# Perceiver block on one core: two mixtures of experts with three float32r products for each fp32 product

## The reference

```python
# stage 5: x is the normalised input, 8 experts, one for each row
logits = x @ gate_w.T
top_v = jnp.max(logits, axis=-1); sel = jnp.argmax(logits, axis=-1)
rw = jax.nn.sigmoid(top_v)
for e in range(n_exp):
    xs = x * (rw * (sel == e))[:, None]
    out = out + (xs @ w_up[e].T) * jax.nn.silu(xs @ w_gate[e].T) @ w_down[e].T

# stage 8: 8 routed experts (two for each row) and 2 shared ones
def _expert(xf, w1, w3, w2):
    return jax.nn.silu(xf @ w1) * (xf @ w3) @ w2
gates = softmax of the two largest logits of each row, 0 elsewhere
out = sum_e gates[:, e] * _expert(xf, routed e) + sum of the two shared experts
```

## Time and profile before

| | |
|---|---|
| median of 3 runs | 1501.59 us (1499.80 to 1501.68) |
| the profiled execution | 1503.77 us, its span 1502.0 us |
| TensorE busy | 95% of the span |
| mean granted TensorE clock | 0.987 of full speed |
| stage 5 (normalisation to the last down) | about 518 to 575 us of the span |
| stage 8 | about 777 to 847 us |

### The profile page before, as it was taken

The page is one execution under the profiler, slowest core; times in us unless marked ns, Lnnn a source line. Parts: engine busy times, 40 slices in busy tenths (PEclk is TensorE's granted clock), DMA queues, the critical chain, the costliest instruction groups (busy, mean ns, idle before and its releaser), DMA issues.

```text
span 1502.0 us, 26221 instructions
## 1 busy us (share of the span) xinstructions
PE 1430.5 (95%) x10513; PEld 979.6 (65%) x10513; DVE 967.1 (64%) x1667; ACT 750.2 (50%) x1379; POOL 331.2 (22%) x439
## 2 busy tenths in 40 slices
PE   7899999999999999999999989999989899999998
PEld 4797666887888655898565545555545454555697
DVE  4776645544787534787363378889989892567533
ACT  5574342113665424664442337777777676325232
POOL 3784340002643213642103041110000000100000
PEclk9999999999999999999999999999999999999999
DMA  9314132221212410211315365545757412310140
GB/s 373 129 57 181 63 121 92 95 85 36 73 69 107 151 59 35 91 57 55 106 70 186 51 173 92 85 76 87 177 79 146 93 20 106 161 57 2 57 169 14
DMA packets 43008, 147.74 MB, mean 98 GB/s; under 512 B 6380, under 2 KB 21996, under 8 KB 34028
## 3 DMA queue, kind: packets, MB, share of 16 engines
q1 hardware_dynamic: 42888, 146.07, 33.7%
HBM read 123.49 MB, written 22.56 MB: 97 GB/s over the span
## 4 chain that ended last, share of the span: by engine, by line
PE 83%; DVE 9%; ACT 4%; issue 2%; POOL 2%; DMA 0%; SPq 0%; ACTq 0%; POOLq 0%; DVEq 0%
PE PS L163 51%; PE PS L2399 8%; PE PS L2311 7%; PE PS L2296 5%; PE PS L634 2%; PE PS L1660 2%; DVE SM L2415 2%; PE PS L1889 1%; POOL CNr L932 1%; PE PS L1910 1%; PE PS L2390 1%; PE PS L2985 1%; PE PS L1917 1%; PE PS L2890 1%; DVE SM L306 1%
## 5 line engine op out<-in xcount | busy, mean ns | idle before, releaser
L2415 DVE TENSOR_REDUCE SM<-PS 128x1 f32<-128x1024 f32 x256 | 301.8, 1219 | 42.4 <-PE PS L2296 41.1
L163 PE MATMUL PS<-ARr 128*128 128x256 f32 (+1 forms) x672 | 177.2, 323 | 0.8 <-POOL CNr L932 0.8
L2311 PE MATMUL PS<-AR 49*128 49x256 bf16 (+1 forms) x1216 | 162.9, 271 | 1.1 <-DVE AR L2436 0.7
L163 PE MATMUL PS<-HT,AR 128*128 128x512 f32 x328 | 153.4, 616 | 2.6 <-ACT HT L355 1.1
L163 PE MATMUL PS<-CNr,ARr 128*128 128x256 f32 x672 | 130.7, 292 | 11.6 <-DVE ARr L801 10.7
L2311 PE MATMUL PS<-AR,CT 49*128 49x256 bf16 (+1 forms) x832 | 124.6, 272 | 0.0
L163 PE MATMUL PS<-ARr,HTr 128*128 128x512 f32 x384 | 122.3, 400 | 0.5 <-issue 0.5
L163 PEld LDWEIGHTS PS<-ARr 128*128 128x128 f32 x672 | 114.9, 190 | 10.1 <-issue 1.2
L862 ACT CAST ARr<-PS 128x512 fp32r<-128x512 f32 x96 | 56.3, 586 | 112.5 <-PE PS L634 112.5
L163 PEld LDWEIGHTS PS<-HT,AR 128*128 128x128 f32 x328 | 61.4, 195 | 78.0 <-issue 74.1
L163 PE MATMUL PS<-AR 128*128 128x256 f32 (+3 forms) x504 | 109.5, 371 | 1.4 <-DVE AR L720 0.8
(11 more groups left out here) (403 smaller groups left out, 2727.7 us busy)
## 6 DMA issues: line engine op xcount, KB each, us to landing
CN<-ctx_n SPq DMA_DIRECT2D x24, 1024.0 KB, 5.6
AR<-k_parts SPq DMA_DIRECT2D x114, 128.0 KB
k_parts<-CN SPq DMA_DIRECT2D x32, 384.0 KB, 3.3
CT<-pack SPq DMA_DIRECT2D x6, 2048.0 KB, 7.6
AR<-pack SPq DMA_DIRECT2D x20, 512.0 KB, 4.6
CT<-k_parts SPq DMA_DIRECT2D x78, 128.0 KB
CT<-ctx_t SPq DMA_DIRECT2D x8, 1024.0 KB, 19.1
v_ones<-CN SPq DMA_DIRECT2D x28, 288.0 KB, 3.0
```

The lines of the kernel that those rows point to most:

```text
L163: last = te.matmul(o, l, r, start=first and k == 0, stop=final and k == n - 1, skip_group_check=True)
L2311: return te.matmul(PS[:, b, z * 256:z * 256 + 256], keys[rows, c * 128:c * 128 + 128], QQ9[rows, pr, rest, cols], start=not rest, stop=boo ...
L2415: ve.tensor_reduce(MX9[:, p % 2, e, g % 8 // 4, g % 4:g % 4 + 1], PS[:, b:b + 2, :].rearrange("p a b -> p (a b)"), AX, ALU.max).then_inc(* ...
```

## The change

In both mixtures gate, up and down of each expert become three float32r products: head of the weight by head of the rows, head by rest, rest by head. Gate 0, up 0 and the last down stay fp32.

- ScalarE casts HT to float32r (HTH) after its half of the turned rows; VectorE subtracts (HTR, two operations) before it copies the logits.
- For gate and up of expert e ScalarE casts both weights (`head_gate_up`, to GUH), and VectorE subtracts (`rest_gate_up`; the rest is written over the weight, W and WR being the same place). For down the same with `head_down` (DH) and `rest_down`.
- For the hidden rows ScalarE casts HB to HBH (in the space of H), and VectorE subtracts to HBR, over HB, at the end of its part for e.
- TensorE's gate e now waits for `gur` e and `htr`, down e for `hr` e and `dr` e.
- Ahead of its loop VectorE does `rest_gate_up` 1, then copies the gate rows, then `rest_down` 0 and `rest_gate_up` 2. ScalarE does `head_gate_up` 1, `head_down` 0, `head_gate_up` 2 at the start of its part.

```diff
-        CT = sb("CT", [128, 2, 8192])
-
         def both(name, shape):
 
             with nc.sbuf_tensor(name, shape, F32) as a:
                 pass
             return a, sb(name + "r", shape, F32R)
 
+        CT, CTr = both("CT", [128, 2, 8192])
         CN, CNr = both("CN", [128, 64, 256])
         X = sb("X", [128, 4, 256])
-        H = sb("H", [128, 4, 256])
+        H, Hr = both("H", [128, 4, 256])
...
-        def experts(s, W, n, n_gated, R, RT, work, gate_first):
+        def experts(s, W, WR, n, n_gated, R, RT, work, gate_first, HTH, HTR, GUH, DH):
             RB = [view(AR, work + 512 * k, 512) for k in range(2)]
             GB = [view(AR, work + 1024 + 512 * k, 512) for k in range(2)]
             HB = [view(AR, work + 2048 + 512 * k, 512) for k in range(3)]
+            HBR = [view(ARr, work + 2048 + 512 * k, 512) for k in range(3)]
+            HBH = [view(Hrf, 512 * k, 512) for k in range(2)]
 
             row_gone = lambda e: ("h", s, "up" if gate_first else "row", e)
             gate_gone = lambda e: ("h", s, "gated" if gate_first else "up", e)
             ready = lambda e: ("h", s, "gated" if gate_first else "row" if e < n_gated else "up", e)
+            late = lambda e: ("late", s) if e >= 5 and not gate_first else ("w", s)
             esel, idb = W["esel"].bitcast(BF16), W["idb"].bitcast(BF16)
+            gu = lambda e, k: mat(GUH[e % 2][:, 256 * k:256 * k + 256], 2)
 
             def pe_part(pe):
                 te = pe.e
 
+                def hidden(e, kind, k, gone):
+                    b, before = PB.take((kind, s, e), gone)
+                    pe.wait_ge(*before, *ht_all(s))
+                    w, o = mat(W[f"{kind}{e}"], 2), PS[:, b, :]
+                    if e == 0:
+                        last = mm(te, o, [(w[:, kt, :], HT[:, kt, :]) for kt in range(2)])
+                    else:
+                        pe.wait_ge(("gur", s, e), ("htr", s))
+                        wh, wr = gu(e, k), mat(WR[f"{kind}{e}"], 2)
+                        last = mm(te, o, [p for kt in range(2) for p in (
+                            (wh[:, kt, :], HTH[:, kt, :]), (wh[:, kt, :], HTR[kt]), (wr[:, kt, :], HTH[:, kt, :]))])
+                    last.then_inc(*pe.inc("expert", kind + "_ps", s, e))
+
                 def gate(e):
-                    wg = mat(W[f"g{e}"], 2)
-                    b, before = PB.take(("g", s, e), ("g", s, e))
-                    pe.wait_ge(*before, *ht_all(s), ("late", s) if e >= 5 and not gate_first else None)
-                    mm(te, PS[:, b, :], [(wg[:, kt, :], HT[:, kt, :]) for kt in range(2)]).then_inc(
-                        *pe.inc("expert", "g_ps", s, e))
+                    hidden(e, "g", 0, ("g", s, e))
 
                 def up(e):
-                    wu = mat(W[f"u{e}"], 2)
-                    b, before = PB.take(("u", s, e), ("h", s, "up", e))
-                    pe.wait_ge(*before)
-                    mm(te, PS[:, b, :], [(wu[:, kt, :], HT[:, kt, :]) for kt in range(2)]).then_inc(
-                        *pe.inc("expert", "u_ps", s, e))
+                    hidden(e, "u", 1, ("h", s, "up", e))
 
                 def down(e):
-                    pe.wait_ge(ready(e))
-                    h = HB[e % 3]
-                    for i in range(4):
-                        z = te.matmul(ACC[i], h[:, tok(i)], W[f"d{e}"], start=e == 0 and i % 2 == 0, stop=e == n - 1,
-                                      skip_group_check=True)
+                    h, d = HB[e % 3], W[f"d{e}"]
+                    if e == n - 1:
+                        pe.wait_ge(ready(e))
+                        for i in range(4):
+                            z = te.matmul(ACC[i], h[:, tok(i)], d, start=False, stop=True, skip_group_check=True)
+                    else:
+                        pe.wait_ge(("hr", s, e), ("dr", s, e))
+                        hh, hr, dh, dr = HBH[e % 2], HBR[e % 3], DH[e % 3], WR[f"d{e}"]
+                        for i in range(4):
+                            z = mm(te, ACC[i], [(hh[:, tok(i)], dh), (hh[:, tok(i)], dr), (hr[:, tok(i)], dh)],
+                                   e == 0 and i % 2 == 0, False)
                     z.then_inc(*pe.inc("expert", "down", s, e))
 
 
...
                     half_pe(pe, f"h{s}", 1)
                 down(n - 1)
 
+            def rows_rest_dve(dv):
+                dv.wait_ge(("hth", s))
+                for kt in range(2):
+                    z = dv.e.tensor_tensor(HTR[kt], HT[:, kt, :], HTH[:, kt, :].bitcast(F32), ALU.subtract)
+                z.then_inc(*dv.inc("rest", "htr", s))
+
             def dve_part(dv):
                 ve = dv.e
+                rest_gate_up(dv, 1)
                 gate_rows_dve(dv, s, RT)
+                rest_down(dv, 0)
+                rest_gate_up(dv, 2)
                 for e in range(n):
                     g, h, rb = GB[e % 2], HB[e % 3], RB[e % 2]
                     h_free = ("down", s, e - 3) if e > 2 else None
...
                         if e < n_gated:
                             dv.wait_ge(("h", s, "up", e), ("rb", s, e))
                             ve.tensor_tensor(h, h, rb, ALU.mult).then_inc(*dv.inc("expert", "h", s, "row", e))
+                    rest_down(dv, e + 1)
+                    if e:
+                        rest_gate_up(dv, e + 2)
+                    if e < n - 1:
+                        dv.wait_ge(("hh", s, e))
+                        ve.tensor_tensor(HBR[e % 3], h, HBH[e % 2].bitcast(F32), ALU.subtract).then_inc(
+                            *dv.inc("rest", "hr", s, e))
                 for q in range(2):
                     x = X[:, 2 * q:2 * q + 2, :].rearrange("p a b -> p (a b)")
                     dv.wait_ge(("down", s, n - 1))
...
                     x_done(dv, s, 2 * q, ("x", s, q))
                     x_done(dv, s, 2 * q + 1, ("x", s, q))
 
+            def rows_head_act(ac):
+                ac.wait_ge(*ht_all(s))
+                ac.e.copy(HTH, HT[:]).then_inc(*ac.inc("head", "hth", s))
+
+            def head_gate_up(ac, e):
+                if e < n:
+                    ac.wait_ge(late(e), ("u_ps", s, e - 2) if e > 2 else None)
+                    ac.e.copy(GUH[e % 2][:, 0:256], W[f"g{e}"])
+                    ac.e.copy(GUH[e % 2][:, 256:512], W[f"u{e}"]).then_inc(*ac.inc("head", "guh", s, e))
+
+            def head_down(ac, e):
+                if e < n - 1:
+                    ac.wait_ge(late(e), ("down", s, e - 3) if e > 2 else None)
+                    ac.e.copy(DH[e % 3], W[f"d{e}"]).then_inc(*ac.inc("head", "dh", s, e))
+
             def act_part(ac):
                 ae = ac.e
+                head_gate_up(ac, 1)
+                head_down(ac, 0)
+                head_gate_up(ac, 2)
                 if gate_first:
                     half_act(ac, f"h{s}", 0)
                 for e in range(n):
...
                     if e < n_gated:
                         ac.wait_ge(("rb_ps", s, e), row_gone(e - 2) if e > 1 else None)
                         ae.copy(rb, bank("rb", s, e)).then_inc(*ac.inc("expert", "rb", s, e))
+                    head_down(ac, e + 1)
                     if gate_first:
                         ac.wait_ge(("g", s, e))
                         ae.activation(g, g, ACT.Silu).then_inc(*ac.inc("expert", "silu", s, e))
+                    if e:
+                        head_gate_up(ac, e + 2)
+                    if e < n - 1:
+                        ac.wait_ge(ready(e), ("down", s, e - 2) if e > 1 else None)
+                        ae.copy(HBH[e % 2], HB[e % 3]).then_inc(*ac.inc("head", "hh", s, e))
                 if gate_first:
                     half_act(ac, f"h{s}", 1)
 
-            return pe_part, dve_part, act_part
+            def rest_gate_up(dv, e):
+                if e < n:
+                    dv.wait_ge(("guh", s, e))
+                    for k, kind in enumerate("gu"):
+                        z = dv.e.tensor_tensor(WR[f"{kind}{e}"], W[f"{kind}{e}"],
+                                               GUH[e % 2][:, 256 * k:256 * k + 256].bitcast(F32), ALU.subtract)
+                    z.then_inc(*dv.inc("rest", "gur", s, e))
+
+            def rest_down(dv, e):
+                if e < n - 1:
+                    dv.wait_ge(("dh", s, e))
+                    dv.e.tensor_tensor(WR[f"d{e}"], W[f"d{e}"], DH[e % 3].bitcast(F32), ALU.subtract).then_inc(
+                        *dv.inc("rest", "dr", s, e))
+
+            return pe_part, dve_part, act_part, rows_rest_dve, rows_head_act
...
+        WR5, _ = placed("s5", ARr, 7443)
+        pe_experts_5, dve_experts_5, act_experts_5, rows_rest_5, rows_head_5 = experts(
+            5, W5, WR5, 8, 8, R5, RT5, 2322, True, view(CNrf, 8192, 2, 512),
+            [view(ARr, 14691, 512), view(ARr, 6930, 512)],
+            [view(ARr, 14179, 512), view(ARr, 5906, 512)],
+            [view(ARr, 15203, 256), view(ARr, 6418, 256), view(ARr, 6674, 256)])
...
             turn_out(dv, 5, "ht", HT, 0)
+            rows_rest_5(dv)
```

(8 more changed lines are left out.)

6 lines of the change are left out of this document (4 added, 2 removed).

## The result

| | before | after |
|---|---|---|
| median | 1501.63 us (6 runs, 1499.80 to 1509.05) | **1486.69 us** (6 runs, 1485.04 to 1491.05) |
| ratio | | 0.9897, 95% interval 0.9878 to 0.9917 |
| the profiled execution | 1503.77 us, span 1502.0 | 1486.03 us, span 1484.2 |
| mean granted clock | 0.987 | 0.988 |

What follows compares the result with a forecast made beforehand. TensorE, busy 95% of the span, was taken as the bound. Gains of 4.3 and 4.6 less 1.5 for the clock gave 7.4 off 1503.77, or 1496.4; 2.2 lower on the median, 1494.2 us, range 1486.8 to 1499.2.

Steps and rivals of the forecast that it cites:

- The mixtures: Stages 5 and 8, the loops over experts: stage 5 gains 4.3 us, stage 8 gains 4.6 us.
- The prices from the cross attention: float32r products on TensorE: six of 512 columns in 1.40 us, twelve of 256 in 1.51 us.
- The failed step: Outside stages 5 and 8: nothing is changed, later stages just begin earlier, so no further gain was counted.
- The clock term of 1.5: TensorE's clock after two new idle times of over 2 us: a loss between 0 and 3 us, taken as 1.5.
- VectorE and GpSimd take turns: Mixture starts: each VectorE subtraction waits for one GpSimd split operation, of 0.61 or 1.17 us.
- Rival B: Mixture starts: GpSimd keeps the ports through its run, VectorE entering at 536.83 and 803.99; 1504.3 us, chance 0.04.
- Rival A: Mixture starts: VectorE slips in before GpSimd, or little is locked; 1486.9 us with the clock spared, chance 0.22.
- The wait before up 1: Start of stage 5: TensorE stands still 2.4 us, until VectorE's first product frees a PSUM bank.
- Steady passes: Both mixtures, one expert's part of the loop: 4.63 us each instead of 5.68, without waits.
- pass 1 (1.3): Stage 8: TensorE idle 1.3 us before the spread product of expert 1's part of the loop.
- gate 3 (0.9): Stage 8: TensorE waits about 0.9 us before expert 3's gate, VectorE being behind by its queue.
- Rival C: Both mixtures: passes cost 5.0 to 5.3 us instead of 4.63, some 4.5 less gain; 1498.8 us, chance 0.12.

Runs made afterwards that it cites:

- one mixture alone: Changed kernel with the new path switched off in the other mixture: only stage 5 changed 1495.47 us, only stage 8 changed 1492.77, beside 1503.47 before.
- early rests: Changed kernel with the first roundings and subtractions made before the routing: 1484.67 us, ratio 0.9873 to the kernel before.
- stage 5 alone: Changed kernel with the new path only in stage 5, stage 8 keeping its fp32 products: 1495.47 us, ratio 0.9943 to the kernel before.
- short splits: Changed kernel with GpSimd's key splits of stages 5 and 8 cut to 8 of 512 columns: 1484.35 us, ratio 0.9873 to the kernel before.

## Why the prediction was wrong, and where it was right

- **The mixtures: right.** Forecast 4.3 and 4.6, measured 4.18 and 4.63, and the same to 0.05 with one mixture alone. The prices from the cross attention carried over: six products of 512 columns in 1.40 us, but for the first, below.
- **The failed step** is the last one of the sum: "Neither before nor behind the mixtures is anything changed; later stages just begin earlier". It put the gain outside the mixtures at nothing, and it was 9.6 us behind stage 8 in the two profiles. The lines are the same, but TensorE's queue is 269 instructions longer, and the pauses of stage 9 stand at one place in blocks of 256: 7.45 us before, 1.26 after. Padding of 13 in the old kernel gave 5.4 us, padding of 243 in the new one brought three of the four pauses back and took 1.5 to 4.7. The row of it was on record, 1.93 us with "issue" as its end; I read it for the clock alone and didn't ask what issue meant there.
- **The clock term of 1.5** also failed: it was subtracted on top. The loss is real: the half-clock stretch of stage 8 costs about 4 x 0.43 = 1.7 us. But it lies inside that stage's 4.63 and replaces other waits that I had counted there. Outside the mixtures the clock took nothing that shows (mean 0.988 after 0.987, which is within what single executions differ by). Behind waits the clock fell after 2.25 us at gate 1 in stage 8 and 1.97 with early rests, and stayed at 1.00 after 1.60 before up 1 in stage 5. Nor did the length decide: of the pauses of stage 9 before, 1.58, 2.01 and the first of 1.93 left it at 1.00 and the second of 1.93 didn't; with stage 5 alone one of 1.51 was followed by half clock. The Trainium skill ("TensorE: Matmul & The Clock Gate", "HAM oscillation") describes a kernel whose clock fell at the wait of every turn of its loop; those waits were longer than these, and here it fell at some only.
- **VectorE and GpSimd take turns: right**, and shown by the short splits. The Trainium skill ("SBUF — State Buffer", "Who interferes with whom") has only the mutual exclusion; here one VectorE operation gets in for about one of GpSimd's. Rival B (GpSimd keeps the ports) is out: the first rests of stage 5 were done at 531.4, 5 us before GpSimd's run ended. Rival A's time, 1486.9, is nearly what was measured, but that is a coincidence: the subtractions did wait.
- **Terms off in size.** The wait before up 1 is 1.6, not 2.4: VectorE was through its queue 0.9 sooner than I counted (its first product ended at 535.46, not 536.35). Steady passes cost 4.74 and 4.70, not 4.63, which over the six passes from pass 1 to 7 of stage 5 takes that back. The 0.11 is one product: from the first of gate and up behind the spread product to the next it is 0.34 us (546.88 to 547.22), and 0.23 from there on. In stage 8 the waits that I had put at pass 1 (1.3) and gate 3 (0.9) were 0 and 0.16, and half clock stood in their place. The sum for the mixtures came out right partly because such errors cancel; that much of the agreement is luck.
- **Rival C (steady passes wait)**: no. They wait 0.

Open: why a block is late and how long it holds TensorE up (behind the 1496th product it is 0.79 us in the first profile of the changed kernel and 2.16 in the second); why 128 more instructions, with one pause in the profile, don't show a gain in the median; and 1.7 of the 9.6 us behind stage 8.

## What to carry to other kernels

When a kernel's TensorE pauses end with "issue", treat the place in its instruction stream as part of the experiment: before crediting a gain of 1% or less to an edit, pad the old kernel so that its instructions lie as in the new one, and compare single stretches of the profiles beside the medians. A wait that two engines cause in series must be attacked at both; one repair alone shows little of the gain (0.4 and 0.6 of 4.0 us here). Operations of GpSimd that stand beside VectorE's SBUF-to-SBUF work are best put where VectorE is idle, not merely where GpSimd is.
